# A two-layer Mamba stage on five engines: z products, mean and variance in earlier places of TensorE's order, five ScalarE steps in other slots

## The reference, cut to what matters

```python
mu = seq.mean(-1, keepdims=True)
var = ((seq - mu) ** 2).mean(-1, keepdims=True)
h = (seq - mu) * jax.lax.rsqrt(var + EPS) * ln_g + ln_b
xs, z = jnp.split(h @ in_w, 2, axis=-1)
xc = jax.nn.silu(causal_conv4(xs) + conv_b)
dbl = xc @ xproj_w
delta = jax.nn.softplus(dbl[..., :6] @ dt_w + dt_b)
dA = jnp.exp(delta[..., None] * A)
dBx = delta[..., None] * B[:, :, None, :] * xc[..., None]
h_t = dA * h_(t-1) + dBx                      # scan along the sequence
y = einsum(h_t, C) + Dp * xc
seq = seq + (y * jax.nn.silu(z)) @ out_w
```

## Time and profile before

| | us |
|---|---|
| median of 3 runs (7573.76 to 7584.95) | 7579.1 |
| the profiled execution | 7586.52 |
| its span | 7584.4 |

### The profile page before, as it was taken

The page is one execution under the profiler, slowest core; times in us unless marked ns, Lnnn a source line. Parts: engine busy times, 40 slices in busy tenths (PEclk is TensorE's granted clock), DMA queues, the critical chain, the costliest instruction groups (busy, mean ns, idle before and its releaser), DMA issues. The chain is left out here.

```text
span 7584.4 us, 105356 instructions
## 1 busy us (share of the span) xinstructions
PE 6025.3 (79%) x18336; PEld 2083.4 (27%) x18336; DVE 6449.6 (85%) x7490; ACT 5235.8 (69%) x10936; POOL 5449.8 (72%) x4289
## 2 busy tenths in 40 slices
PE   6877878878878883688888888888888777898686
PEld 2222222222222221222222222222222113488252
DVE  6999999999999997299999999999999994533636
ACT  6777777777777773477877787777777774322756
POOL 5888888888888883288888898888888881000606
PEclk8999999999999996788999999999998888997888
DMA  3444454444445445487887888888787873246322
GB/s 87 115 106 101 108 112 104 103 112 112 101 104 115 107 100 125 116 188 180 186 188 184 187 189 186 187 185 186 183 187 183 182 167 96 105 154 195 82 60 77
DMA packets 584410, 1051.09 MB, mean 139 GB/s; under 512 B 105735, under 2 KB 140733, under 8 KB 579101
## 3 DMA queue, kind: packets, MB, share of 16 engines
q1 hardware_dynamic: 584060, 1047.70, 58.4%
HBM read 857.89 MB, written 189.54 MB: 138 GB/s over the span
## 5 line engine op out<-in xcount | busy, mean ns | idle before, releaser
L1624 POOL TENSOR_TENSOR scan_prod<-scan_hs,scan_BC_rep 128x512 f32<-128x512 f32 x1536 | 1941.1, 1270 | 326.0 <-DVE scan_hs L1548 316.6
L644 POOL TENSOR_TENSOR mamba_prod<-mamba_hs,mamba_BC_rep 128x512 f32<-128x512 f32 x1536 | 1904.9, 1272 | 34.8 <-DVE mamba_hs L602 29.3
L602 DVE TENSOR_TENSOR_SCAN mamba_hs<-mamba_dA,mamba_carry,mamba_dbx 128x512 f32<-128x512 f32 x1152 | 1436.1, 1271 | 39.7 <-ACT mamba_carry L530 19.4
L1173 PE MATMUL scan_u_rep<-scan_du,scan_sel 96*128 96x512 f32 x1536 | 942.9, 698 | 539.1 <-DVE scan_hs L1548 539.0
L526 ACT ACTIVATE mamba_dA<-mamba_delta_rep,mamba_a_neg 128x512 f32<-128x512 f32 x1536 | 1088.8, 710 | 216.6 <-DMA mamba_delta_rep<-delta_units 116.1
L1398 ACT ACTIVATE scan_dA<-scan_delta_rep,scan_a_neg 128x512 f32<-128x512 f32 x1536 | 1092.5, 712 | 98.0 <-DVE scan_hs L1548 87.0
L1548 DVE TENSOR_TENSOR_SCAN scan_hs<-scan_dA,scan_carry,scan_dbx_even 128x512 f32<-128x512 f32 x768 | 976.7, 1272 | 47.9 <-ACT scan_carry L1378 33.6
L1548 DVE TENSOR_TENSOR_SCAN scan_hs<-scan_dA,scan_carry,scan_u_rep 128x512 f32<-128x512 f32 x768 | 977.4, 1273 | 38.2 <-ACT scan_carry L1378 34.4
L581 DVE TENSOR_TENSOR mamba_dbx<-mamba_u_rep,mamba_BC_rep 128x512 f32<-128x512 f32 x1152 | 780.7, 678 | 83.8 <-PE mamba_u_rep L325 53.4
L336 PE MATMUL mamba_y<-mamba_prod,mamba_gather 128*32 128x512 f32 x3072 | 593.3, 680 | 322.7 <-POOL mamba_prod L644 322.7
L1947 POOL TENSOR_TENSOR ffn_sq<-ffn_xm 96x512 f32<-96x512 f32 x64 | 66.2, 1034 | 952.2 <-DVE ffn_xm L1915 941.8
(11 more groups left out here) (283 smaller groups left out, 10458.3 us busy)
## 6 DMA issues: line engine op xcount, KB each, us to landing
scan_BC_rep<-proj_rows SPq DMA_DIRECT2D x1024, 256.0 KB, 6.5
scan_delta_rep<-proj_rows SPq DMA_DIRECT2D x1024, 192.0 KB, 3.6
mamba_BC_rep<-bc_units SPq DMA_DIRECT2D x512, 256.0 KB, 7.5
mamba_delta_rep<-delta_units SPq DMA_DIRECT2D x512, 192.0 KB, 5.5
proj_rows<-scan_dbc SPq DMA_DIRECT2D x256, 224.0 KB, 3.3
delta_units<-mamba_delta SPq DMA_DIRECT2D x128, 192.0 KB, 5.7
by_n<-fin_res SPq DMA_DIRECT2D x32, 768.0 KB, 3.2
fmid_src<-by_n SPq DMA_DIRECT2D x32, 768.0 KB, 5.1
```

The costliest lines, as they stand in the source:

```text
L602: nc.vector.tensor_tensor_scan(hs[:, s % RING_H], dA[:, s % RING_A], dbx_bank(s)[:], carry[:, bass.ds(at, 1)], op0=ALU.mult, op1=ALU.add). ...
L644: pool.tensor_tensor(prod[:, (G * u + s) % RING_P], hs[:, s % RING_H], BC_rep[:, u, QUADS + s % QUADS], ALU.mult).then_inc(s_prod, 1)
L1173: nc.tensor.matmul(u_rep[c][:], sel[:, c], du[:, k], start=True, stop=True).then_inc(s_rep_u, 1)
L1624: pool.tensor_tensor(prod[:, (G * k + s) % RING_P], hs[:, (G * k + s) % RING_H], BC_rep[:, k, 2 + s % 2], ALU.mult).then_inc(s_prod, 1)
```

## The change

On TensorE the second z half moves from slot 23 to slot 22, where it follows the first; the mean moves from slot 2 to slot 0 and the variance from slot 5 to slot 2. On ScalarE: the square from slot 7 to 6, rsqrt from 9 to 10, silu from 10 to 12, copy_bc and the first softplus half from 13 to 14, the second half from 14 and 15 to 15 and 16, `affine` from 16 to 17, the copy of the sums (second half) from slot 6 to 9 and the output copy from 12 to 13. VectorE, GpSimd and SyncE keep their lists.

```diff
             def ahead_step(s, lay, m, v):
-                if s == 2:
+                if s == 0:
                     mean(m, v)
-                elif s == 5:
+                elif s == 2:
                     var(m, v)
                 elif 14 <= s < 22:
                     convolve(lay, m, (s - 14) // K, (s - 14) % K)
-                elif s >= 22:
-                    project_z(lay, m, s - 22)
+                elif s == 22:
+                    for j in range(2):
+                        project_z(lay, m, j)
...
-                elif s == 10:
+                elif s == 12:
                     silus(m, v)
-                elif s == 13:
+                elif s == 14:
                     copy_bc(m)
...
-                elif s == 14:
+                elif s == 15:
                     softplus_begin(lay, m, 1)
-                elif s == 15:
+                elif s == 16:
                     softplus_end(m, 1)
...
-                if s == 7:
+                if s == 6:
                     square(m)
-                elif s == 9:
+                elif s == 10:
                     rsqrt(m)
-                elif s == 16:
+                elif s == 17:
                     affine(lay, m)
...
-                    if s == 6 and prev is not None:
+                    if s == 9 and prev is not None:
                         evict_y(n - 1, 1)
...
-                    if s == 12 and prev is not None:
+                    if s == 13 and prev is not None:
                         evict_out(n - 1)
```

## The result

| | before | after |
|---|---|---|
| time, median of 4 runs each, same chip | 7580.61 us (7573.76 to 7584.95) | 7661.73 us (7635.8 to 7668.66) |
| profiled execution, span | 7584.4 us | 7666.5 us |
| busy share of the span: DVE, PE, POOL, ACT | 85, 79, 72, 69% | 84, 80, 71, 68% |
| first scan to last scan of the Mamba stage | 2833.8 us | 2916.0 us |

The ratio is 1.0096, 95% interval [1.0084, 1.0109]: the change costs 81 us between the medians and 73 by the ratio, where a gain of 51 was forecast. All of it lies in the Mamba stage, whose first to last scan grew by 82.2 us in the profiles.

A forecast was written before the change was run, and what follows sets the result against it. VectorE was taken to wait on a ring through the last z copy, 44.37 us a unit. A mean of 43.55 saves 0.82 over 62 units, 51 us: 7535.5 profiled, 7528 us on the median's scale; range 7497 to 7581.

The forecast's parts named there:

- Where VectorE's lost time is: Mamba stage: VectorE loses some 116 us, 33 at its loop heads and 83 waiting for ScalarE in slots 11 to 17.
- The ring through the last z copy: ScalarE's z copy, softplus, GpSimd's products, TensorE's sums, next z copy: this cycle sets the pace, 44.37 us a unit.
- the 33 us booked as VectorE's own pause: VectorE issues nothing at 26 loop heads, up to 1.43 us each; taken as 33 us, untouched by the change.
- the 83 us of the ring: VectorE's waits for `dA` or `carry` of ScalarE in slots 11 to 17; 83 us, of which 80 recoverable at full clock.
- The new wait on PE costs nothing while that cover stands.: TensorE slot 22: z half 1 waits for `raw` half 1, copied three microseconds before the sums can start; cost zero.
- The new slots of ACT ... the price is nothing.: ScalarE's later slots bind only by VectorE: `dA` of slot 17 ends at 27.3 us, needed at 29.5; no cost.
- The mean over slow and full-clock turns: Turns swing between 41.4 and 44 to 45 us; mean 43.55 a unit, gaining 0.82 over 62 units, 51 us.
- the slow stretch stays: Rival: TensorE's clock still halves at the sums, new ring 44.2 to 44.4 us, no gain, about 7577 us; chance 0.16.
- two slow stretches in one unit: Rival: clock halves at projections and sums, ring 47.6 us; with one unit in four, 42 us lost, 7621; chance 0.08.
- It would be wrong if DVE waited for a spread of PE in slot 3: A sign named beforehand as refuting the forecast: VectorE's slot 3 waiting for TensorE's spread; no size given.
- Closes another ring: Earlier mean and variance shorten the cycle mean, square, silu, projections, softplus, GpSimd, sums to 41.4 us, or 44.2 at half clock.
- The half of the throttled time: Skill's clock rule: 5.7 us at 0.50 would cost 2.85 us a unit, 177 us over 62; not used in the sum.

The follow-up runs named there:

- E7: The kernel before with all loops of the Mamba stage written out as plain code for each unit: 7588.53 us, ratio 1.0008.
- E5: The changed kernel with ScalarE's loop over unit pairs alone written out, other engines keeping theirs: 7580.78 us, ratio 0.9999.
- E2: The kernel before with both z products in slot 22 as the only edit, loops kept: 7583.62 us, ratio 1.0008.
- E1: The changed kernel with z half 1 put back in TensorE's slot 23, the rest of the change kept: 7713.92 us, ratio 1.0176.
- E12: The changed kernel with all of ScalarE's slots as before, TensorE's new order and the loops kept: 7539.5 us, ratio 0.9935.
- E13: The changed kernel with silu back from slot 12 to 10 and rsqrt from 10 to 9: 7544.84 us, ratio 0.9943.
- E14: The changed kernel with the square back from slot 6 to 7 and the copy of the sums from 9 to 6: 7648.94 us, ratio 1.0078.
- E17: The changed kernel with one redundant spread of the input on TensorE in slot 7, ahead of the projections: 7575.46 us, ratio 0.9997.
- E18: The changed kernel with two redundant spreads of the input on TensorE in slot 7, ahead of the projections: 7573.63 us, ratio 0.9992.

## Why the prediction was wrong

**Where VectorE's lost time is.** Half right. The ring through the last z copy and its 44.37 us held to the digit, even with the loops written out (E7), though with other legs. But the 33 us booked as VectorE's own pause and the 83 us of the ring were not two terms: with the pauses gone the time stayed.

**"The new wait on PE costs nothing while that cover stands."** This step failed. The cover was read at the head of a first-layer iteration, 1044.71 to 1045.38 against sums at 1048.41. At the head of the second layer's iterations ScalarE issues nothing for 7 us, the copy comes at 2050.91, after the loop body's first scan began at 2050.53, and the wait is 5.91 us. The prediction looked for a loop pause on VectorE alone, though the same waits view had 84.9 us of it on ScalarE. E5 prices the pause: 81 us, the whole difference to before. The z move's own part in it is less: in E2 the second layer lost 33 us where the first gained 24, and in E1, with z half 1 back, the second layer loses 36 us more than the first, by a way that was not traced.

**"The new slots of ACT ... the price is nothing."** This failed too, and by most: 122 us (after less E12), 117 of them silu's (after less E13). The working tested the slots against VectorE's schedule and found 2 us of room, but had itself put silu into the ring: its 10.2 us from `xm` to silu's end, measured 10.24, were 7.63 before (1013.90 to 1021.53). With them the ring is 44.8 at half-clock projections, above VectorE's 42.48. Of the 2.6 us, two slots of `dA` and `carry`, 1.4, are silu's; the rest, 1.2, is the square's slot and the copy of the sums, and taking those out (E14) gave back 13 us. With silu's 1.4 out (E13) the first layer takes 1468.66 us, 43.2 a unit, with projections still partly slow (813 ns in the mean). So a microsecond in the ring is not worth the same wherever it stands; why the square's part is worth so little was not tested.

**The mean over slow and full-clock turns.** The terms of the ring were right to some tenths (10.24 for 10.2; 7.23 for 4.04 + 3.4; 3.05 for 3.06; 19.76 for 0.16 + 19.62), only PE's part at the mean was 5.90 in this turn, between its 4.3 and 7.1; it was 4.2 to 4.3 in 20 of the 24 turns from 300 to 1400 us. The average, the term that gave the 51 us, was not: 43.55 a unit was assumed, since some units were to have no slow stretch. Measured are 1509.78 / 34 = 44.4 in the first layer, for two reasons. Slow projections came in 24 of 25 units, not in some. And a turn below VectorE's 42.48 was counted as a gain, while the trace shows ScalarE waiting for the scans behind it (41.31, then 46.72 us). The rival "the slow stretch stays" describes the first layer: the old ring replaced by one as long, no gain.

**The rival "two slow stretches in one unit"** had the right sign, with a chance of 0.08, and a wrong cause. What made it slower was a pause of ScalarE that no case named. "It would be wrong if DVE waited for a spread of PE in slot 3" is what came.

**"Closes another ring"** for the mean: the ring exists (75.0 us of `xm` waits in 24 units of the first layer), but the early mean gains 44 us by the medians, 55 by the ratios, with ScalarE's old slots (E2 to E12). It is an edit to keep.

**The clock.** The page TensorE: Matmul & The Clock Gate of the Trainium skill, section "A second HAM failure mode: psum-queue depth-cycling", tells of a kernel in which frequent small idle times between groups of matmuls make the clock swing. This case agrees in part: in the change a gap of 1.66 us ahead of the projections goes with a granted 0.52, and filling it brings the clock back (E17, E18). But the projections of E2 are slow with no gap ahead of them (834 ns, 0.0 us). The half of the throttled time, which the prediction took from the section "HAM oscillation", is not the price here: in E7 the projections lose 1.7 us a unit to the clock (5.37 against 3.67) and the ratio is 1.0008. What counts is whether the ring comes out above VectorE's pace.

**What stays open:** why ScalarE pauses near 7 us at the heads of the second layer's loop and not at those of the first; why VectorE's own pause grew from 1.4 us to 2.5 with the change (27.7 us in 11 from 300 to 1400 us) and has but two rows, of 1.4 us, in E12 (300 to 3000 us); what lets the clock fall at the projections; and E13 with ScalarE's loop written out, which was not run.

## What to carry to other kernels

Before an edit is priced at nothing because another wait covers it, look for the iteration in which that wait is latest, at each loop's head and on each engine; a pause that costs nothing in a kernel paced by a ring (E7) does cost time once the ring is open or something stands behind it. When an order closes a ring close to the bound engine's pace, a slot inside the ring can cost time however much room its own consumer has: write the ring's sum in both clock levels, keep the worse one below the pace, and count no gain for turns shorter than the pace. Test the parts of a change apart before it is dropped whole: here two parts of three were worth 44 us with the loops kept and 102 with them written out, and one line (silu's slot) hid it.

## What was not expected of the hardware

- A loop's head is not free, and not alike on all engines and loops: ScalarE issued nothing for 6.8 us in the mean, ten times in 1000 us in the second layer, with no such row in the first (300 to 1400 us); VectorE for 1.4 us in the mean before and for up to 3.4 us in the change, in both layers.
- A matmul whose result nobody needs made the changed kernel 86 us faster (E17); one matmul of the eight passes behind it fell from 916 to 699 ns in the mean.
- A gap of 2.04 us ahead of the projections left the clock at 1.00 in the kernel before, and one of 1.66 us at the same place went with 0.52 in the changed one. In E7, which has the order of the kernel before on every engine, 1.91 us went with 0.68. So the length of the last gap alone does not tell.
